# Attention and mixture-of-experts kernel: the router's product behind the transpose of the row maxima, and the split of the maxima on GpSimd

## The reference

```python
x = x + xattn(layernorm(x), ctx)      # 8 heads of 8 channels, rotary positions, softmax over 256 keys
x = x + ffn(layernorm(x))             # 16 experts, top 2 of each token by a router, and a shared expert
# attention of a batch and head: softmax(q k^T / sqrt(8)) v, then Wo and bias
# router: softmax(xt @ Wr.T + bias), the two largest, normalised to a sum of 1
# expert: (silu(x Wg) * (x Wu)) Wd, hidden width 128; rows x are the 4096 tokens of 256 numbers
```

## Time and profile before

| what | value |
|---|---|
| median of three executions | 881.02 us (879.29 to 883.98) |
| the profiled execution | 880.23 us, of which the span of the profile is 878.4 us |
| mean granted TensorE clock | 0.945 of full speed |
| VectorE busy | 627.2 us, 71% of the span |
| ScalarE busy | 512.1 us, 58% |
| GpSimd busy | 450.4 us, 51% |
| TensorE, products | 743.0 us, 85%, by modelled ends |

### The profile page before, as it was taken

One profiled execution on the slowest core, in us unless ns is written; L12 is line 12 of the kernel. 1 busy time (PEld: TensorE's weight loads), 2 busy tenths in 40 slices (PEclk: granted clock), 3 DMA queues, 4 the chain that ended last, 5 costly groups with the idle time before them and its releaser, 6 DMA issues. The chain is left out here.

```text
span 878.4 us, 23052 instructions
## 1 busy us (share of the span) xinstructions
PE 743.0 (85%) x6138; PEld 530.9 (60%) x6139; DVE 627.2 (71%) x1653; ACT 512.1 (58%) x1213; POOL 450.4 (51%) x929
## 2 busy tenths in 40 slices
PE   3699999999999999999999999962899299999900
PEld 2356666766766666666666666531566188888700
DVE  6877898898899888888888899638333134444467
ACT  3155777777777777777777777651555045555400
POOL 5444555645645555555564563122777535656510
PEclk9999999999999999999999999985799799999965
DMA  8597344444444444444434469720222345555379
GB/s 255 137 301 220 107 125 122 105 128 124 109 120 113 125 114 118 123 106 129 121 105 127 123 177 287 237 68 1 97 106 106 124 117 153 145 155 156 98 227 347
DMA packets 112404, 126.46 MB, mean 144 GB/s; under 512 B 14189, under 2 KB 98928, under 8 KB 112369
## 3 DMA queue, kind: packets, MB, share of 16 engines
q1 hardware_dynamic: 105456, 109.11, 45.0%
q0 software_dynamic: 6912, 16.93, 5.2%
HBM read 76.93 MB, written 50.63 MB: 145 GB/s over the span
## 5 line engine op out<-in xcount | busy, mean ns | idle before, releaser
L797 DVE TENSOR_REDUCE M<-bank_s 128x2 f32<-128x512 f32 x512 | 339.7, 685 | 60.6 <-PE bank_s L1050 55.3
L600 ACT ACTIVATE Pr<-bank_st 128x512 f32<-128x512 f32 x512 | 295.6, 598 | 122.9 <-PE bank_st L1078 117.8
L1050 PE MATMUL bank_s<-QK 72*128 72x256 bf16 x1024 | 201.4, 280 | 13.1 <-DMA QK<-parts 11.1
L1078 PE MATMUL bank_st<-QK 98*128 98x256 bf16 x1024 | 197.8, 275 | 1.3 <-ACT Pr L600 1.1
L1033 PE MATMUL bank_o<-Pr,wide 128*32 128x256 f32 x2048 | 139.5, 388 | 0.0
L1050 PEld LDWEIGHTS bank_s<-QK 72*128 72x128 bf16 x1024 | 93.3, 102 | 70.7 <-DVE M L797 34.3
L525 POOL TENSOR_TENSOR work<-work 128x256 f32<-128x256 f32 x64 | 46.8, 731 | 162.6 <-DVE work L855 162.6
L940 DVE TENSOR_TENSOR OT<-work,bank_st 128x128 f32<-128x128 f32 x112 | 32.2, 288 | 136.2 <-ACT work L681 136.2
L1078 PEld LDWEIGHTS bank_st<-QK 98*128 98x128 bf16 x1024 | 97.8, 98 | 27.4 <-ACT Pr L600 4.6
L571 POOL DMA_INDIRECT results<-QK,ids_out x80 | 78.4, 980 | 64.9 <-issue 49.4
L1184 PE MATMUL bank_st<-wgu,xT_sb 128*128 x320 | 84.4, 387 | 0.0
(11 more groups left out here) (145 smaller groups left out, 1218.5 us busy)
## 6 DMA issues: line engine op xcount, KB each, us to landing
QK<-parts SPq DMA_DIRECT2D x128, 288.0 KB
parts<-parts_sb SPq DMA_DIRECT2D x128, 96.0 KB, 2.3
slots<-xT_sb SPq DMA_DIRECT2D x8, 1300.0 KB, 6.3
wide<-slots SPq DMA_DIRECT2D x80, 130.0 KB, 2.3
ctx_kv<-ctx_dram SPq DMA_DIRECT2D x64, 128.0 KB, 2.1
QK<-results SPq DMA_DIRECT2D x16, 512.0 KB, 8.2
X<-x_dram SPq DMA_DIRECT2D x8, 512.0 KB, 7.8
parts<-parts_sb SPq DMA_DIRECT2D x64, 64.0 KB, 2.1
```

The source lines that it names most:

```text
L600: nc.scalar.activation(Pr[k][:], bank_st[k % 2][:], ACT.Exp, scale=SCALE).then_inc(s_exp, 1)
L797: nc.vector.tensor_reduce(M[:, c, 2 * k:2 * k + 2], bank_s[S_BANK[c][k]][:].rearrange("p (a s) -> p a s", a=2), AX.X, ALU.max).then_inc(s_ ...
L1050: last = nc.tensor.matmul(bank_s[S_BANK[at.mod(2)][k]][:, T * t:T * t + T], Q[c][0:KR, k, P * t:P * t + P], K[c][0:KR, k, :], start=True, ...
L1078: last = nc.tensor.matmul(bank_st[k % 2][:, T * s:T * s + T], K[c][0:MROW + 2, k, P * s:P * s + P], Q[c][0:MROW + 2, k, :], start=True, st ...
```

## The change

GpSimd gets the split at the head of its step; instead of a copy it subtracts a zero (`newton[:, 2:3]`, a column of zeros read for all 16 columns). VectorE loses both operations. On TensorE the router's product moves from k = 1 to k = 2, behind the transpose of `Mb` and ahead of `values(at, 1)`.

```diff
@@ GpSimd
             def step(at):
+                if at.has(1):
+                    c = at.mod(2, 1)
+
+                    wait(pool, s_red, at.value(8, 16))
+                    wait(pool, s_TM, at.value(1, 0))
+                    nc.gpsimd.tensor_tensor(Mb[:, c, 0, :], M[:, c, :], newton[:, 2:3].to_broadcast([P, 2 * H]),
+                                            ALU.subtract).then_inc(s_hi, 1)
+                    wait(pool, s_hi, at.value(1, 2))
+                    nc.gpsimd.tensor_tensor(Mb[:, c, 1, :], M[:, c, :], Mb[:, c, 0, :],
+                                            ALU.subtract).then_inc(s_msp, 1)
                 if at.r % 2 == 0 and at.has(-4):
@@ VectorE
-                    if k == 0 and at.has(1):
-                        c = at.mod(2, 1)
-
-                        wait(dve, s_red, at.value(8, 16))
-                        wait(dve, s_TM, at.value(1, 0))
-                        nc.vector.tensor_copy(Mb[:, c, 0, :], M[:, c, :]).then_inc(s_hi, 1)
-                        wait(dve, s_hi, at.value(1, 2))
-                        nc.vector.tensor_tensor(Mb[:, c, 1, :], M[:, c, :], Mb[:, c, 0, :],
-                                                ALU.subtract).then_inc(s_msp, 1)
@@ TensorE
                                             ident_b[:]).then_inc(s_TM, 1)
-                    if k == 2 and at.has(-1):
-                        values(at, 1)
-                    if even and k == 1 and at.has(-6):
+                    if even and k == 2 and at.has(-6):
 
                         if at.i is None and at.r == 6:
                             pe.wait_ge(s_wr, 32)
@@
                                                     start=(c == 0), stop=(c == 1))
                         last.then_inc(s_lg, 1)
+                    if k == 2 and at.has(-1):
+                        values(at, 1)
                     if k == 4 and at.has(-1):
```

## The result

The changed kernel takes 893.4 us (median of four executions: 891.56, 892.98, 893.83, and one in the chip's slower state, 1103.34, that the comparison leaves out), the kernel before 881.71 beside it: a ratio of 1.0136, 95% interval 1.0109 to 1.0162. It is slower by 1.4%. The profiled execution took 891.56 us with a span of 889.8, which is 11.3 us more than the one before (891.56 - 880.23).

The account below looks back on a forecast made before the run. No engine's share named a bound, so attention was read as TensorE's beats, 16.79 us a pair of steps. Pairs +14.6, last pairs -0.8, first steps +0.8 gave 895.6 us against the median 881.02, 8-in-10 range 882.5 to 905.

Parts of the forecast that it names:

- The ring in the odd half: From odd-step to even-step transpose of `Mb`: rotary products, five GpSimd operations and split lead to the transpose, 8.37 us.
- The moved product: Router's product between transpose and value products in the even half: 0.22 + 0.36 + 0.20, taken as 0.77 us more.
- The sign of 0.2 us idle ahead of the value products: If the prediction was right, TensorE would idle 0.2 us between the router's product and the value products.
- The hidden chain: Newton's chain on GpSimd, even half: earlier guess, chain ends near 4.1 us after the beat, rotary products at 4.4.
- T_even: Start of TensorE's transpose of `Mb` in an even step, used as a beat; the even half starts there.
- The regular pairs: 26 pairs of steps in the attention part: each 17.35 us instead of 16.79, together +14.6 us.
- The last four beats: Two pairs of steps behind the 26, without the five GpSimd operations: about -0.4 us each, -0.8 us.
- The early steps: First steps, where the split comes behind GpSimd operations ending after the transpose: +0.8 us, range 0 to 1.9.
- GpSimd doesn't close the odd half: Rival: split ready before TensorE, odd half 7.62 us, pair 16.60, -5 us, 876 us; chance 0.07.
- The rival without switches: Rival: the array switches around the router's product cost nothing; even half 8.57, pair 16.94, +3.9 us, 885; chance 0.13.
- the third rival: A 16-column GpSimd operation costs 0.45 us, not 0.22; odd half 8.83, even 9.09, +29 us, 911; chance 0.10.
- The fourth, no effect: Rival: something both kernels share holds the rhythm and the exchange of waits is even; 881 us; chance 0.10.

Follow-up runs that it names:

- third_op: Changed kernel with one more GpSimd operation of 16 columns, whose result nobody reads, ahead of the split; 905.45 us in one execution.
- early_split: Changed kernel with the GpSimd split ahead of the last of the five operations, one step earlier in the program; ratio 0.9883 to the kernel before, on another chip.
- split_only: Changed kernel with the router's product put back to k = 1, the split staying on GpSimd; 888.59 us, ratio 1.0087 to the kernel before.
- router_only: Changed kernel with the split put back on VectorE, the router's product staying behind the transpose; 877.7 us, ratio 0.9959 to the kernel before.
- early_ahead: Changed kernel with the GpSimd split ahead of the last of the five operations and the router's product ahead of the transpose; 862.58 us, ratio 0.9813.
- third_wide: third_op plus one f32 product of 256 columns ahead of the transpose in even steps; 951.14 us on a chip where the kernel before took 939.36.
- third_half: third_wide with the wide product in every second even step alone; 968.54 us on a chip where the kernel before took 939.36.

## Why the prediction was right

**Sign and size.** Forecast 895.6 us, 1.7% slower; measured 893.4 and 1.4%. It was inside the range, and the likeliest case came. The size is partly luck, as shown under what missed.

**The ring in the odd half** was 8.37 by the sum and 8.36 in the trace. Its new term was the split: 0.22 us an operation by the straight line between 1 and 256 columns, 0.217 measured. The Trainium skill ("GPSIMD Engine Reference", "Elementwise — side-by-side cycle accounting") gives about 2.6 cycles per element, from which the prediction estimated the same 0.22, and the trace agrees. Overlap (0.04) and gap (0.08) were kept. Two small terms missed and cancelled: from the split's end to the transpose it was 0.05 us (410.44 to 410.49), not the 0.12 borrowed from VectorE, and the five operations began 0.16 after the rotary products (these ended at 406.27), not 0.08. third_op (+0.18 in, +0.18 out) and early_split show the cause, in both directions.

**The moved product** was to add 0.77 in the even half; it added 0.69 to 8.20. The two distances behind it were nearly right (0.16 for 0.22, 0.55 for 0.56). What was mis-sized was their meaning: I charged 0.36 for the product and 0.41 for the switches, and the experiments give 0.50 and 0.19. (The three terms 0.22 + 0.36 + 0.20 add up to 0.78; the sum carried 0.77 on.) The sign of 0.2 us idle ahead of the value products did not come: at the two new switches the loads are idle for 0.07 and 0.03 us (410.58 to 410.65, 411.17 to 411.20). The Trainium skill ("TensorEngine Tiling (Array Packing)", "Key Properties") states that TensorE drains at a change of tiling. The trace agrees at the switches that both kernels have, with 0.21 and 0.41 us of idle time; two more of them cost less than these rows suggest, perhaps since work behind a pause catches up.

**The hidden chain.** The prediction said that the guess comes at T_even + 0.2 and Newton's chain no longer delays the five operations. The trace has the first Newton operation at 410.79, 0.3 after the beat; the chain ends at 414.49, and the five operations start at 414.89, released by VectorE's rotary products. split_only shows what happens without it: 0.42 us more in the even half.

**What missed.** The sum was 14.6 - 0.8 + 0.8 = 14.6 us; the trace has 11.3. The regular pairs gave 12.0 for 14.6, 0.10 less per pair: 0.09 in the even half (8.89 for 8.98) and 0.01 in the odd. The rest is small and in part the clock's. The last four beats gave -2.7 for -0.8, but 1.4 of it is the fall at 553.0 in the kernel before. Against split_only, which has the product at k = 1 too and no fall there (30.71), the changed kernel's 29.62 is 1.1 less: the moved product brings about what the sum had. The early steps were to cost 0.8 and came out 2.3 faster. The first T_even lies between 96.5 and 102.2 us over all kernels run; the three without a fall between 60 us and that beat (changed, router_only, early_ahead) have 96.5 to 98.3, the eleven others 98.0 to 102.2. So the fall at 82.0 in the kernel before may be most of the 2.3, and the term itself isn't readable. The expert part gave +1.1 for nothing; from the last transpose of `Mb` to the end it varies between 307.9 and 311.3 us among the kernels on the first two chips, though none of them changes it. The two falls in the pairs added 3.3 us that no case of the prediction held, and the falls in the kernel before took nearly as much off again. That this came out even is luck; by the regular pairs alone the change costs 12.0 us, not 14.6.

**The rivals.** "GpSimd doesn't close the odd half" is what early_split builds. It is faster by 1.2%, where the rival's sum had 0.6%; its odd half is the rival's 7.62. The rival without switches needed an even half of 8.57; even behind the value products it is 8.70. An operation of 16 columns costs 0.217, not the third rival's 0.45 (whose 881 + 29 us are 910, not 911). The fourth, no effect, has fallen with the regular pairs, 17.25 for 16.79.

## What to carry to other kernels

Take one repeating event on the busiest in-order engine as a beat, and price a change half by half: what is removed from one half and added to the other doesn't cancel when another engine closes the first. Before work moves to an idle engine, look at what stands ahead of it in that engine's order, and put the short operation that somebody waits for ahead of the long one that nobody waits for (0.74 us a pair here). Where an engine has to wait, put independent work right ahead of the wait, not behind it: the same product cost 0.69 us behind the transpose and nothing ahead of it, as long as the wait was there (0.44 us in the other half once it was gone). And before a difference of a few us is explained, the granted clock is to be read stretch by stretch in both kernels.

## What the runs showed of the hardware that was not expected

- TensorE's granted clock fell behind some beats to its lower level for 3.4 us, 1.6 us lost each time, though TensorE was idle for only 1.0 to 1.2 us there. Two products of 16 columns in the gap didn't prevent it (2 and 6 falls, as without them). With one f32 product of 256 columns there was none (none behind 26 beats in third_wide, none behind the 13 beats that have it in third_half), though the loads were idle for longer at the transpose than with the small products. TensorE's busy time doesn't show the difference: it fills the hit halves and the others alike. The traces show this in one execution of each kernel.
- Two extra switches between whole-array and quarter-array products cost 0.19 us, though the switches that were there before show 0.21 or 0.41 us of idle time each.
- A VectorE operation of 16 columns takes 0.16 to 0.20 us, or up to 0.68 where it starts while a GpSimd operation of 256 columns runs: each one over 0.4 us ended 0.03 us after the GpSimd operation did (32 in the kernel before, 45 in router_only). On GpSimd the same operation takes 0.21 to 0.22 every time.
